# A two-layer graph kernel: three reorderings on ACT's queue, in the setup, in turn 1 and at a block's end

## What is computed

```python
# layer 0: graph attention
h = relu(layernorm(x))
Wh = h @ W;  f1 = Wh @ a1;  f2 = Wh @ a2
e = leaky_relu(f1 + f2.T, 0.2)
att = softmax(where(adj > 0, e, -9e15), axis=-1)
x = x + relu(att @ Wh)
# layer 1: node-conditioned weights, then the adjacency
h = relu(layernorm(x))
node = h @ W1                                  # 8192 x 16
hw = einsum('nc,kcf->nkf', h, W2)
m = einsum('nk,nkf->nf', node, hw)
x = x + relu(adj @ m + node @ b)
```

## Time and profile before

| | |
|---|---|
| time, median of 3 runs | 1773.1 us (1770.45 to 1778.39) |
| the profiled execution's own time | 1749.66 us |
| its span (first to last instruction) | 1747.9 us |
| PE busy | 1701.2 us (97%) |
| DVE, ACT, POOL busy | 1290.1, 1089.2, 548.7 us |
| mean granted clock of TensorE | 0.994 of full |
| DMA, whole span | 452.23 MB, mean 259 GB/s |

### The profile page before, as it was taken

One profiled execution on the slowest core, in us unless ns is written; L12 is line 12 of the kernel. 1 busy time (PEld: TensorE's weight loads), 2 busy tenths in 40 slices (PEclk: granted clock), 3 DMA queues, 4 the chain that ended last, 5 costly groups with the idle time before them and its releaser, 6 DMA issues.

```text
span 1747.9 us, 35898 instructions
## 1 busy us (share of the span) xinstructions
PE 1701.2 (97%) x11311; PEld 1468.8 (84%) x11311; DVE 1290.1 (74%) x1775; ACT 1089.2 (62%) x1889; POOL 548.7 (31%) x522
## 2 busy tenths in 40 slices
PE   8889899999999999999999999999999999999998
PEld 5789788888888988988888888898777788888886
DVE  8679688888888898888888888888566443533534
ACT  5554466767666677676676767663655655555554
POOL 0000044454453544544445445355444200000000
PEclk9999999999999999999999999999999999999999
DMA  9999999999999999999999999987533345453430
GB/s 236 280 347 367 324 279 315 298 328 303 292 321 310 300 315 307 306 303 313 311 295 312 320 291 315 311 245 288 208 140 145 122 171 193 154 204 144 168 144 24
DMA packets 316753, 452.23 MB, mean 259 GB/s; under 512 B 21072, under 2 KB 291616, under 8 KB 298912
## 3 DMA queue, kind: packets, MB, share of 16 engines
q1 hardware_dynamic: 164928, 228.63, 44.2%
q10 hardware_dynamic: 144944, 203.58, 39.0%
q0 software_dynamic: 6832, 19.41, 3.4%
HBM read 364.46 MB, written 87.07 MB: 258 GB/s over the span
## 4 chain that ended last, share of the span: by engine, by line
PE 81%; DMA 5%; SPq 4%; DVE 3%; issue 2%; ACTq 2%; ACT 1%; POOL 1%; DVEq 0%; POOLq 0%
PE ot_ps L820 42%; PE ot_ps L877 13%; PE mt_ps L877 13%; PE hw_ps L789 12%; SPq L295 3%; DMA maskT_d<-mt 2%; ACTq L295 2%; DMA xt<-in_x_dram 1%; ACT wh_mask L529 1%; DMA adj_sb<-in_adj_dram 1%; PE h_ps L784 1%; SPq L310 1%; DVE att L985 1%; DVE p_sb L1009 1%; POOL prod L406 1%
## 5 line engine op out<-in xcount | busy, mean ns | idle before, releaser
L820 PEld LDWEIGHTS ot_ps<-wh_mask,p_sb 128*128 128x128 f32 x8192 | 945.7, 193 | 84.6 <-issue 69.8
L820 PE MATMUL ot_ps<-wh_mask,p_sb 128*128 (+1 forms) x8192 | 954.7, 277 | 25.6 <-DVE p_sb L1009 20.7
L1009 DVE SCALAR_TENSOR_TENSOR p_sb<-zb,qcol,mt 128x1024 f32<-128x1024 uint8 (+1 forms) x512 | 729.7, 1442 | 17.9 <-DVE mt L933 10.0
L529 ACT ACTIVATE wh_mask<-adj_sb 128x2048 uint8<-128x2048 f32 x256 | 485.2, 1921 | 70.3 <-issue 53.4
L406 POOL TENSOR_TENSOR prod<-prod 128x1024 f32<-128x1024 f32 (+2 forms) x192 | 333.8, 1739 | 567.8 <-ACT prod L595 550.6
L1057 DVE CAST mask<-adj_sb 128x1024 fp32r<-128x1024 uint8 x272 | 204.0, 757 | 244.9 <-PE mt_ps L877 243.2
L622 ACT ACTIVATE mask<-adj_sb 128x1024 fp32r<-128x1024 uint8 x240 | 255.2, 1064 | 173.8 <-PE ot_ps L877 173.6
L595 ACT ACTIVATE prod<-hw_ps,node 128x128 f32<-128x128 f32 x1024 | 278.7, 383 | 113.2 <-PE hw_ps L789 111.7
L877 PE MATMUL mt_ps<-mask,msgs 128*128 128x512 f32 x1024 | 282.6, 398 | 2.1 <-DVE mask L1057 1.1
L877 PE MATMUL ot_ps<-mask,msgs 128*128 128x512 f32 x1024 | 274.7, 390 | 1.1 <-DVE mask L1057 0.5
L789 PE MATMUL hw_ps<-wcat,hT 128*128 128x512 f32 x512 | 240.7, 592 | 0.0
(11 more groups left out here) (108 smaller groups left out, 575.4 us busy)
## 6 DMA issues: line engine op xcount, KB each, us to landing
adj_sb<-in_adj_dram SPq DMA_DIRECT2D x536, 256.0 KB, 7.7
adj_sb<-in_adj_dram ACTq DMA_DIRECT2D x488, 256.0 KB, 8.9
maskT_d<-mt ACTq DMA_DIRECT2D x64, 1024.0 KB, 10.3
adj_sb<-maskT_d SPq DMA_DIRECT2D x32, 2048.0 KB, 7.7
keep_d<-keep POOLq DMA_DIRECT2D x64, 128.0 KB, 6.0
p_sb<-keep_d SPq DMA_DIRECT2D x4, 2048.0 KB, 12.0
msg_d<-msg POOLq DMA_DIRECT2D x56, 128.0 KB, 5.8
msgs<-msg_d SPq DMA_DIRECT2D x7, 1024.0 KB, 9.0
```

Source lines behind the costliest of these rows:

```text
L529: ins = act.activation(m8[:, q // 2, 2 * (q % 2) + part, :], adj_sb[:, q, part * T * COLS:(part + 1) * T * COLS], ACT.Copy, scale=EDGE)
L820: ins = pe.matmul(ot_ps[h][:, (t - t0) * ROW:(t - t0 + 1) * ROW], p_sb[:, r, t * P:(t + 1) * P], rows, start=begin and t == t0, stop=end a ...
L1009: dve.scalar_tensor_tensor(p_sb[:, r, :], zbf[:, bass.ds((ib % 2) * BLK, BLK)], qcol[:, bass.ds(tile + b_, 1)], mtb[:, p, k // 2, :, 2 * ( ...
```

## The change

Three edits, all in ACT's queue.

1. Setup: the cast of buffer 2's first part moves from before the exponentials' table load to behind the copies of `zb`, next to the second part.
2. `xt` of block 0 is loaded in turn 1, half 0, step 2, and no longer in the last half of block 0. In the later blocks it stays.
3. In a block's last half `load_upper(i + 2, 2)` stands behind `copy_sums` and no longer ahead of it.

```diff
--- before.py
+++ after.py
@@ -546,7 +546,7 @@
                 if i + 1 < NB:
                     relu_x(i + 1)
                 take_wh(i)
-                if i >= 3:
+                if 3 <= i < 7:
                     cast((i - 3) // 2, (i - 3) % 2, 1, 0)
             act.activation(std[:, :], eps[:, :], ACT.Exp)
             act.wait_ge(setup_dve, 13)
@@ -558,7 +558,8 @@
                 act.wait_ge(z0_done, h + 1)
                 act.activation(zbf[:, h * HB:(h + 1) * HB], hw_ps[h][:, :], ACT.Copy).then_inc(z0_copied, 1)
 
-            cast(2, 1, 1, 0)
+            for part in range(2):
+                cast(2, part, 1, 0)
             act.activation(std[:, :], eps[:, :], ACT.Sqrt)
             act.wait_ge(setup_pe, 8)
             act.activation(whsum[:, :], h_ps[:, 0:D], ACT.Copy).then_inc(setup_act, 1)
@@ -631,19 +632,22 @@
                             if isinstance(i, int) and i == 0 and p == 0:
                                 load_upper(1, 2)
                             load_upper(i + 1 + p, 3 - 2 * p)
-                        if k == 3:
+                        if k == 3 and not (ends_block(jg) and p == 1):
                             load_upper(i + 2, 2 * p)
                         if k == 0:
                             act.wait_ge(squared, A * n + A)
                             act.dma_start(maskT_d[bass.ds(2 * jg + p, 1), bass.ds(ib, 1), :, :]
                                           .rearrange("s i p w -> (s i p) w"),
                                           mt[:, p, :, :].rearrange("p c n -> p (c n)")).then_inc(mt_stored[p], 16)
-                        if ends_block(jg) and p == 1 and k == 2:
+                        if finish and ends_block(jg) and p == 1 and k == 2:
                             load_xt(ib)
+                        if isinstance(i, int) and i == 1 and p == 0 and k == 2:
+                            load_xt(0)
                         if ends_block(jg) and p == 1 and k == 3:
                             if last:
                                 convert(0, True, 0)
                             copy_sums(ib)
+                            load_upper(i + 2, 2)
                         ahead = None if last else lambda: cast(2 * p, 1, i + 2, A * n + A)
                         if finish:
                             u = i - IT
```

## The result

| | before | changed |
|---|---|---|
| time, median of 22 runs each | 1756.42 us | 1763.62 us |
| ratio, changed to before | | **1.0059** (95%: 1.0034 to 1.0084) |
| the profiled execution's own time | 1749.66 us | 1759.23 us |
| span | 1747.9 us | 1757.5 us |
| mean granted clock | 0.994 | 0.992 |

The change made the kernel 0.6% slower, some 10 us, where 0.4% faster was forecast.

What follows compares the result with a forecast made beforehand. PE was taken as the bound, busy 1701.2 of 1747.9 us, so only its gaps and slow stretches could be won. Terms 0 + 1.8 - 8.7 + 0 = -6.9 took the median 1773.1 to 1766.2 us; range 1759 to 1778.

Steps and rivals of the forecast that it cites:

- Edit 3, the ends of blocks 1 to 6: Ends of blocks 1 to 6: moved issues pass the copies, finish near 346, delay no prod; 0 us (-1.8 to +1.2).
- Rival B: Ends of blocks 1 to 6: copies hold ACT's queue, prods 2.2 late, 1.4 a block lost; sum +4.2 us; chance 0.10.
- Edits 2 and 3, the end of block 0: Block 0's end: copies wait for PE alone, clock stays up, std at 199.9; -8.7 us (-9.2 to -5.1).
- Edit 1: Setup: table load and Exp come 1.4 earlier, but PE's lead is lost at its first stall; 0 us (-1.4 to +0.5).
- Edit 2, xt in turn 1: Block 0, turn 1: the xt load's bytes and issue delay ACT's queue; +1.8 us (0 to 3.4).

Runs made afterwards that it cites:

- only two issues behind: Changed kernel with edit 3 at block 0's end alone, and there two of the four load issues behind the copies; ratio 0.9992 to the kernel before.
- x in two pieces: Changed kernel with the second x loaded in two pieces, tiles 0 and 1 half a turn earlier; ratio 1.0146 to the kernel before.
- two behind at all ends: Changed kernel with two of four load issues ahead of the copies again, two behind, at every block's end; 0.9956, again 0.9982, to the kernel before.

## Why the prediction was wrong

The median, 1763.6, lies inside the forecast range of 1759 to 1778, but by luck: 22 runs put the kernel before at 1756.42 and not at 1773.1. Against its own baseline the change was to give -6.9 us, with ends of -12.4 and 0.0, and gave some +10.

**Edit 3, the ends of blocks 1 to 6: forecast 0, measured +8.2.** This is the step that failed. It said: "Moved behind the copies, the issues should pass them as well and be over near 346." They started at 347.76, with the third copy, and ended at 350.57, and what was priced at 0 cost 1.36 a block through std. Rival B had the mechanism and its size: prods 2.2 late (measured 2.4), 0.8 of slack, 1.4 a block (1.36). Its case against itself, that four activations were passed at 342.51, was named with the right doubt ("those were not waiting for a block's last matmul"), and that doubt deserved more than 0.10. The Trainium skill (Perfetto Trace Analysis, section "DVE / Act Engine Instruction (TENSOR_ADD, Activation, etc)") lets the sequencer fetch on while an activation waits; no run here shows an issue doing so past one whose semaphore is down, and the rows above show it waiting; the measurement decides.

**Edits 2 and 3, the end of block 0: forecast -8.7 (-9.2 to -5.1), measured -6.2.** The same error again, and rival B's 6.0 was nearly right: the working let ACT issue the four loads from 188.6 to 192, ahead of the copies. They went behind them, 197.76 to 200.68, the casts and std followed late (10.97 after the last matmul, forecast 9.9), and PE idled 3.84 in two pieces, after which the clock was low for a group. The rest held: no gap at the boundary, no wait for xt, the next four issues in 3.60 (forecast 3.7). A slip in the sum is small beside this: casts done at 195.7 and issues of 3.7 make 199.4 for std, not 199.9. With only two issues behind, the place gave 8.1.

**Edit 1: forecast 0, measured 0** (1.0001, 0.997 to 1.0033). The mechanism is as told: in the changed kernel the table is loaded at 51.05 and the first Exp starts at 54.54 (forecast 51 and 54.5). The first attention matmul starts at 58.8 to 59.6 in the twelve profiles with the edit, and at 60.9 to 66.0 in the six without; the stalls of block 0 take the lead back. PE waits 11.5 in block 0 before, 13.9 with edit 1 alone and 17.4 in the changed kernel, whose four longest stalls are these, against 3.09 and 2.81 in the earlier trace rows:

```profile
82.79 9.80 PE L824 MATMUL ot_ps<-wh_mask,p_sb 128*128 x64 [4.73 <-DVE p_sb L1013]
97.57 9.26 PE L824 MATMUL ot_ps<-wh_mask,p_sb 128*128 x64 [4.97 <-DVE p_sb L1013]
109.59 3.83 PE L824 MATMUL ot_ps<-wh_mask,p_sb 128*128 x32 [2.76 <-DVE p_sb L1013]
142.21 8.04 PE L824 MATMUL ot_ps<-wh_mask,p_sb 128*128 x55 [2.77 <-DVE p_sb L1013]
```

**Edit 2, xt in turn 1: forecast +1.8 (0 to 3.4), not settled.** Twelve profiles of kernels that load xt in turn 1 end block 0's last matmul between 187.9 and 202.8, 197.1 in the mean; six of kernels that don't end it between 190.0 and 194.8, 192.9 in the mean. The difference of the means is 4.2 with a standard error of 1.4 (an estimate from the scatter of these eighteen), so the load there does seem to cost something, but 1.8 and 4.2 are not told apart, and edit 1 is in ten of the twelve and in two of the six. Of the 7.7 between the two profiles shown much is scatter and no price of the edit. Edit 2 alone (0.9986) and with edit 3 at block 0 (0.9992) say that its gain and its cost together are within 0.6% of nothing.

**What stays open.** Six times 1.36, less the 6.2 at block 0's end and with some 4 for edit 2, makes 0.3 to 0.4%, and edit 3 at the six ends alone 0.5%. The intervals of the changed kernel (1.0059) and of edit 3 at the six ends (1.0071) take this in; those of the same instructions again (1.0102), of edit 3 alone (1.0144) and of x in two pieces (1.0146) don't. Two things were seen that can carry the rest. The first is single blocks in which x lands late. In the second measurement of the changed kernel, block 5 took 151.44. DVE, then PE and the table of the stretch at its start:

```profile
805.40 0.39 DVE L998 TENSOR_TENSOR keep<-att,xt 128x128 f32<-128x128 f32 x1 [5.40 <-DMA xt<-in_x_dram]
```

```profile
808.26 3.81 PE L828 MATMUL ot_ps<-wh_mask,p_sb 128*128 128x129 f32 x16 [2.86 <-DVE p_sb L1017]
```

```profile
808.00:817.00 9.00, 8.73 (x41) 7.78 (x42) 8.84 (x12) 4.36 (x9) 2.54 (x5) 0.65 1.07 353
```

The wait for x is 5.40 instead of 2.4 to 2.8, PE idles 2.86, and its clock is granted at 0.65, partly the lower of its two levels, for the 9 us behind. DVE waited for x 7.2 in one place before, 13.4 in five in the changed kernel, 19.1 in six with edit 3 at the six ends alone and 36.8 in six with edit 3 alone. But kernels that measured no slower waited as long in their profiles: 12.8 with edit 2 alone, 16.0 with edits 1 and 2 and edit 3 at block 0 alone, 19.5 with two behind at all ends. And x in two pieces took nearly all of these waits away and still measured 1.0146. There the second thing shows, TensorE's clock. PE at the starts of blocks 2 and 3 of that kernel, and the table of both stretches:

```profile
360.25 2.70 PE L834 MATMUL ot_ps<-wh_mask,p_sb 128*128 128x129 f32 x16 [0.79 <-DVE p_sb L1025]
...
509.50 2.05 PE L834 MATMUL ot_ps<-wh_mask,p_sb 128*128 128x129 f32 x16 [0.79 <-DVE p_sb L1025]
```

```profile
357.00:366.00 9.00, 7.33 (x37) 5.46 (x36) 7.38 (x10) 5.29 (x10) 5.12 (x8) 0.81 1.08 333
506.00:515.00 9.00, 7.35 (x51) 5.89 (x50) 7.14 (x10) 6.52 (x15) 5.37 (x8) 1.00 1.08 341
```

PE waited the same in both, 0.89 + 0.79 and 0.86 + 0.79, but behind the first the clock was granted at 0.81, partly the lower level, and block 2 took 149.27 where block 3 took 147.76. So a wait that costs 1.36 by itself costs 1.5 more where the clock falls with it. In this profile it fell at the starts of blocks 2, 4, 6 and 7 and not of 3 and 5, in the changed kernel's own profile at none of blocks 2 to 7; how often it falls over all runs is not known, so the size of the rest stays open.

## What to carry to other kernels

A DMA issue behind an activation that waits for another engine's last result started here only when that result was there, and then all that stood behind it in the queue waited for the issues' full time; behind activations whose semaphores were up it started ahead of them. So before issues are moved behind a wait, ask what follows them in the same queue and how much slack that has: here 0.8 us took two issues of 0.73 and not four. And where a kernel's start hangs on loads, one profile of it says little: mark off the steady part, and time the rest.

## What the runs showed of the hardware

- An issue on ACT's queue took about 0.73 from start to start at the ends of blocks (0.58 and its register steps), four together 2.81 to 2.92, and around block 0's end before the change 3.32 and 6.25. It started with prods and a cast still ahead at 342.51, ahead of two copies whose semaphores were up at 193.02, and only with the third copy, whose semaphore had just come up, at 347.76 and 498.55.
- The same instructions ended block 0 anywhere between 187.9 and 202.7 us (the changed kernel's program up to there, in five profiles: 187.9, 192.3, 197.6, 197.7, 202.7).
- TensorE's clock fell after short waits too: 16 matmuls took 3.62 after 3.05 + 0.79 of idle, 3.81 after 2.86, but 2.05 after 1.56 and after 1.07 + 0.79. After 0.86 to 0.89 + 0.79 they took 2.05 at 509.50 and 2.70 at 360.25 in one profile, so the length of the wait alone doesn't decide.
- Beside POOL's fold (353.02 to 358.55 in the changed kernel) DVE's add of x, 0.29 at 648.31 without it, took 2.03 at 353.50; that the fold is the cause was not tested.
